# Output projection of a cross-attention block by Strassen's seven block products per head pair, on one Trainium2 core

## The reference, cut to what matters

```python
x = x + xattn(layernorm(x), ctx)       # x, ctx: (16, 256, 512)
    q, k, v = x @ Wq / sqrt(128), ctx @ Wk, ctx @ Wv   # 16 heads of 128
    c = softmax(q @ k.T) @ v           # (16, 256, 16*128)
    return c @ Wo                      # Wo: (2048, 512)
x = x + ffn(layernorm(x))              # gate, up, silu, down, 512 -> 2048 -> 512,
                                       # operands quantised in blocks of 32
```

## Time and profile before

| | us |
|---|---|
| median of 3 runs (lowest, highest) | 2065.28 (2062.91, 2065.92) |
| the profiled execution | 2064.3 |
| its span, first to last instruction | 2062.7 |

### The profile page before, as it was taken

The page is one execution under the profiler, slowest core; times in us unless marked ns, Lnnn a source line. Parts: engine busy times, 40 slices in busy tenths (PEclk is TensorE's granted clock), DMA queues, the critical chain, the costliest instruction groups (busy, mean ns, idle before and its releaser), DMA issues. The chain is left out here.

```text
span 2062.7 us, 45755 instructions
## 1 busy us (share of the span) xinstructions
PE 2023.9 (98%) x15430; PEld 1506.2 (73%) x15430; DVE 1537.7 (75%) x3339; ACT 1000.6 (49%) x2683; POOL 740.0 (36%) x882
## 2 busy tenths in 40 slices
PE   7999999999999999999999999999999999999998
PEld 6778888788888888878888888888888874444443
DVE  6667777777777777778777777776656558888886
ACT  7865545455555555545555545555555453222232
POOL 5322333333323233333332333331111006777776
PEclk9999999999999999999999999999999999999999
DMA  7734444444444444444444444433333273454554
GB/s 234 201 85 83 90 90 90 87 88 89 91 90 90 91 90 91 89 82 90 89 90 91 90 91 88 90 83 75 70 70 69 55 169 77 81 88 86 88 88 79
DMA packets 455038, 193.26 MB, mean 94 GB/s; under 512 B 418400, under 2 KB 431200, under 8 KB 454848
## 3 DMA queue, kind: packets, MB, share of 16 engines
q1 hardware_dynamic: 432496, 139.26, 35.1%
q0 software_dynamic: 16016, 45.23, 9.0%
q10 hardware_dynamic: 6336, 6.29, 1.0%
HBM read 61.21 MB, written 27.26 MB: 43 GB/s over the span
## 5 line engine op out<-in xcount | busy, mean ns | idle before, releaser
L1091 PE MATMUL b_qk<-kvT,attn_weights 128*128 128x256 f16 x3072 | 377.1, 273 | 13.0 <-DVE qk L760 12.3
L651 ACT ACTIVATE prob<-b_s,nmax 128x256 f32<-128x256 f32 x514 | 239.3, 470 | 290.8 <-DVE nmax L921 290.8
L1091 PE MATMUL b_qk<-xT,attn_weights 128*128 128x256 f16 x3072 | 377.2, 273 | 0.0
L1091 PE MATMUL b_v<-attn_weights,kvT 128*128 128x256 f16 x3072 | 377.2, 273 | 0.0
L1091 PEld LDWEIGHTS b_qk<-kvT,attn_weights 128*128 128x128 f16 x3072 | 299.5, 98 | 104.6 <-issue 18.9
L948 DVE SCALAR_TENSOR_TENSOR psplit<-prob,rrec,psplit 128x256 f16<-128x256 f32 x514 | 306.4, 637 | 79.2 <-ACT psplit L661 79.2
L760 DVE SCALAR_TENSOR_TENSOR qk<-b_qk,qk 128x512 f16<-128x512 f32 x256 | 176.7, 690 | 246.3 <-ACT qk L610 236.6
L610 ACT ACTIVATE qk<-b_qk 128x512 f16<-128x512 f32 x256 | 152.5, 596 | 422.5 <-PE b_qk L1091 422.2
L1091 PEld LDWEIGHTS b_qk<-xT,attn_weights 128*128 128x128 f16 x3072 | 300.6, 98 | 34.7
L1091 PEld LDWEIGHTS b_v<-attn_weights,kvT 128*128 128x128 f16 x3072 | 300.6, 98 | 34.8
L661 ACT ACTIVATE psplit<-prob,rrec 128x256 f16<-128x256 f32 x514 | 233.0, 500 | 68.7 <-DVE rrec L941 68.7
(11 more groups left out here) (132 smaller groups left out, 2643.7 us busy)
## 6 DMA issues: line engine op xcount, KB each, us to landing
ffn_w<-wffn SPq DMA_DIRECT2D x48, 256.0 KB, 2.8
acc<-xtok POOLq DMA_DIRECT2D x16, 512.0 KB, 4.9
out<-acc POOLq DMA_DIRECT2D x16, 512.0 KB, 3.2
xrow<-xtok POOLq DMA_DIRECT2D x31, 256.0 KB, 3.2
out<-attn_weights POOLq DMA_DIRECT2D x31, 256.0 KB, 4.4
kvrow<-kvt POOLq DMA_DIRECT2D x61, 128.0 KB, 2.4
stage<-wattn SPq DMA_DIRECT2D x12, 512.0 KB, 4.0
ffn_scratch<-ffn_t SPq DMA_DIRECT2D x48, 128.0 KB, 2.3
```

What stands on the lines that cost most here:

```text
L651: last = eng.activation(half(prob, q, 256), half(bS, q, 256), ACT.Exp, bias=nmax[:, q:q + 1], scale=1.0, accum_out=rsum[:, q:q + 1])
L1091: last = eng.matmul(out, l, r, start=(a == 0), stop=(a == len(pairs) - 1))
```

## The change

From batch 2 on (`FAST`), the projection of a head pair is no longer 2 x 2 x 2 block products but Strassen's seven, m1 to m7, each of a 128 x 128 combination of context blocks and a 128 x 256 combination of weight blocks, each still three matmuls. The seven products are summed over the batch's 8 pairs in PSUM (`b_pt`, `b_x`, `b_o`, half of `b_w`), and DVE adds them with their signs into `acc`, 12 additions of 256 columns per batch in three groups.

- Context: ACT evicts it whole as f32 into `blocks` (in place of `cbuf`, L106); POOL forms five sums per pair in three instructions (`left_sums`), ACT writes the hi of all seven combinations (`left_hi`, 896 columns), DVE their lo (`left_lo`, 896 columns); the lo of the context (`cbuf`, twice per pair) goes.
- Weights: in batch 1 SP loads the 8 pairs' weights again, POOL, ACT and DVE form and split seven combinations of each (`out_sums`, `out_hi`, `out_lo`; 1792 columns per pair) and SP stores them to DRAM. Later SP brings 6 of 8 pairs back for each batch, in two loads of 512 and 384 KB, into two alternating slots; two pairs stay.
- The quantisation of feed-forward weights moves from quads 4 to 51 to quads 8 to 55. Its code, and that around it, is otherwise the same, but for `store_x1`, which POOL issues one quad later.
- Gate and up use `b_qk`, `b_s`, `b_v`, `b_c`; the steps between attention and feed-forward are reordered; the last additions come one per half tile.

The diff, cut to its core, eight columns of indentation and blank lines left out. Left out are buffer layouts, `slot_w`, `left_part` and the like (views of the new buffers), and loop bounds.

```diff
-FFN_FROM, FFN_TO = QPB, QPB + FFN_TILES
+FFN_FROM, FFN_TO = 2 * QPB, 2 * QPB + FFN_TILES
...
+FAST = 2
+FAST_PAIR, FAST_HEAD = 8 * FAST, 16 * FAST
+PREP = (0, 4, 1, 2, 3, 5, 6, 7)
+RESIDENT = {0: 0, 4: 1}
+RING = {1: 2, 2: 3, 3: 2, 5: 3, 6: 2, 7: 3}
+PART_COLS = (2048, 1536)
...
+LEFT = {"a0": 0, "b1": 1, "a0+b1": 2, "a0+b0": 3, "a1+b1": 4, "b0-b1": 5, "a0-a1": 6}
+TERMS = (("m1", "a0+b1", 3), ("m3", "a0", 2), ("m4", "b1", 1), ("m2", "a1+b1", 0)), \
+    (("m5", "a0+b0", 4), ("m7", "b0-b1", 6), ("m6", "a0-a1", 5))
+OPENS, CLOSES = ("m1", "m4", "m5", "m6"), ("m3", "m2", "m7", "m6")
...
-gate = [bPT, bQK]
-up = [bX, bV]
+gate = [bQK, bS]
+up = [bV, bC]
+product_at = {"m1": bPT[:, 0:256], "m3": bPT[:, 256:512], "m4": bX[:, 0:256], "m2": bX[:, 256:512],
+              "m5": bO[:, 0:256], "m7": bO[:, 256:512], "m6": bW[:, 0:256]}
...
+def slot_use(u):
+    b, p_ = u // 8 - FAST, u % 8
+    if p_ in RESIDENT:
+        return RESIDENT[p_], 1
+    uses = [v for v in RING if RING[v] == RING[p_]]
+    return RING[p_], b * len(uses) + uses.index(p_) + 1
...
+    def load_out(j):
+        c, pc = (PREP[j] // 2 + 1) % QPB, O_AT[PREP[j] % 2]
+        eng.dma_start(wall_ffn[:, :], wattn[c * PIECES + pc]).then_inc(sm["wo_loaded"], 16)
+    def store_out(j):
+        eng.wait_ge(sm["wo_lo"], j + 1)
+        eng.dma_start(wos[PREP[j]], wo_split).then_inc(sm["wo_stored"], 16)
+    def load_slot(u, part):
+        slot, _ = slot_use(u)
+        at = slot * 3584 + part * PART_COLS[0]
+        eng.wait_ge(sm["wo_stored"], 16 * (PREP.index(u % 8) + 1))
+        eng.dma_start(oall[:, at:at + PART_COLS[part]],
+                      wos[u % 8, :, part * PART_COLS[0]:part * PART_COLS[0] + PART_COLS[part]]
+                      ).then_inc(sm[f"slot_loaded{slot}{part}"], 16)
...
+    begin = {0: 2 * 1 + 6, 4: 2 * 3 + 6, 1: 2 * 5 + 6, 2: 2 * 6 + 6}
+    fills = {}
+    for p_, step in begin.items():
+        for part in range(2):
+            fills.setdefault(FAST_HEAD - 16 + step + part, []).append((FAST_PAIR + p_, part, FAST_HEAD - 20 + step))
...
+    def fill(i):
+        for u, part, done in fills.get(i, ()):
+            eng.wait_ge(sm["o_done"], done)
+            load_slot(u, part)
...
+            transpose_p(i, k % 2)
...
+            if i == 4 * QPB - 1:
+                load_out(0)
+            if QPB <= n < 2 * QPB and k % 2:
+                j = 2 * (n - QPB) + k // 2
+                store_out(j)
+                if j < 7:
+                    load_out(j + 1)
+            fill(i)
...
+    def out_sums(j):
...
+        eng.tensor_tensor(wo_sums[:, 0:2, :], wo_rows[:, 2:4, :], wo_rows[:, 0:2, :], ALU.subtract
+                          ).then_inc(sm["wo_sum"], 1)
+        eng.tensor_tensor(wo_sums[:, 2:4, :], wo_rows[:, 0:4:2, :], wo_rows[:, 1:4:2, :], ALU.add
+                          ).then_inc(sm["wo_sum"], 1)
+        eng.tensor_tensor(wo_cross, wo_rows[:, 0, :], wo_rows[:, 3, :], ALU.add).then_inc(sm["wo_sum"], 1)
+    def left_sums(n, k):
+        wait_apart(eng, "c_hi", 4 * n + k + 1)
...
+        eng.tensor_tensor(blocks[:, 4:6, :], blocks[:, 1:9:7, :], blocks[:, 0:4:2, :], ALU.add
+                          ).then_inc(sm["s_sum"], 1)
+        eng.tensor_tensor(blocks[:, 6:8, :], blocks[:, 0:2, :], blocks[:, 2:9:6, :], ALU.subtract
+                          ).then_inc(sm["s_sum"], 1)
+        eng.tensor_tensor(blocks[:, 3, :], blocks[:, 1, :], blocks[:, 2, :], ALU.add).then_inc(sm["s_sum"], 1)
...
+            fast = not isinstance(s, int) or 4 * n >= FAST_HEAD + 4
+            if fast:
+                left_sums(n, 0)
+            if outs:
+                out_sums(2 * q)
             if prepare:
                 prep(n, 2 * s + q // 2, q % 2)
+            if outs:
+                out_sums(2 * q + 1)
+            if fast:
+                left_sums(n, 2)
+            if q == 1 and not first_s:
+                store_x1(s - 1, slot)
             if ffn:
                 round_ffn(n - FFN_FROM)
             if q == 0 and not first_s:
-                store_x1(s - 1, slot)
                 if not isinstance(s, int) or s > 1:
                     x_rescale(2 * s - 3)
...
+    left_sums(NQ, 0)
     x_rescale(2 * B - 3)
+    left_sums(NQ, 2)
...
-            if last_batch and v == 0:
+            if last_batch and v == 3:
                 store_x1(B - 1, acc[:, 0:2 * D].rearrange("p (t d) -> p t d", t=2))
...
-        eng.wait_ge(sm["o_done"], 4 * quads - 4)
...
+    def evict_rows(n, k):
+        i = 4 * n + k
+        eng.wait_ge(sm["c_done"], i + 1)
+        if k % 2 and not (isinstance(n, int) and i == FAST_HEAD + 3):
+            eng.wait_ge(sm["s_lo"], 2 * n + (k - 3) // 2 - FAST_PAIR)
+        at = blocks[:, 1:9:7, :] if k % 2 else blocks[:, 0:4:2, :]
+        eng.activation(at, bC[:, 0:256].rearrange("p (q f) -> p q f", q=2), ACT.Copy, scale=C_OUT
+                       ).then_inc(sm["c_hi"], 1)
+    def left_hi(n, k):
+        u = 2 * n + k // 2 - 2 - FAST_PAIR
+        eng.wait_ge(sm["s_sum"], 3 * (u + 1))
...
+        eng.activation(left_part(k // 2, 0).rearrange("p (n f) -> p n f", f=P), blocks[:, 1:8, :], ACT.Copy,
+                       scale=1.0).then_inc(sm["s_hi"], 1)
...
+    def out_hi(j):
+        eng.wait_ge(sm["wo_sum"], 3 * (j + 1))
...
+        to = wo_part(0)
+        eng.activation(to[:, 0:5:4, :], wo_rows[:, 0:4:3, :], ACT.Copy, scale=W_SCALE)
+        for a in range(2):
+            eng.activation(to[:, 1 + 4 * a:3 + 4 * a, :], wo_sums[:, 2 * a:2 * a + 2, :], ACT.Copy, scale=W_SCALE)
+        eng.activation(to[:, 3, :], wo_cross, ACT.Copy, scale=W_SCALE).then_inc(sm["wo_hi"], 1)
...
-            if front or k < 3:
+            if (front or k < 3) and fast(n, k, 3):
+                evict_rows(n, k)
+            elif front or k < 3:
                 hi(half(cbuf, 2 * head_slot(k), 256), bC[:, 0:256], C_OUT, "c_done", i + 1, "c_hi")
...
+            if (front or k < 3) and k % 2 == 0 and fast(n, k, 4):
+                left_hi(n, k)
+            if isinstance(n, int) and n == NQ and k == 2:
+                silu(0, 1)
+            if outs and k % 2:
+                out_hi(2 * (n - QPB) + k // 2)
...
+    def left_lo(n, k):
+        eng.wait_ge(sm["s_hi"], 2 * n + k // 2 - 1 - FAST_PAIR)
+        eng.tensor_tensor(left_part(k // 2, 1).rearrange("p (n f) -> p n f", f=P), blocks[:, 1:8, :],
+                          left_part(k // 2, 0).rearrange("p (n f) -> p n f", f=P), ALU.subtract
+                          ).then_inc(sm["s_lo"], 1)
+    def out_lo(j):
+        eng.wait_ge(sm["wo_hi"], j + 1)
+        to, hi_part = wo_part(1), wo_part(0)
+        pairs = [(to[:, 0:5:4, :], wo_rows[:, 0:4:3, :], hi_part[:, 0:5:4, :])]
...
+        for dst, rows, above in pairs:
+            last = eng.scalar_tensor_tensor(out=dst, in0=rows, scalar=W_SCALE, in1=above,
+                                            op0=ALU.mult, op1=ALU.subtract)
+        last.then_inc(sm["wo_lo"], 1)
...
+    def add_products(b, group):
+        c = b - FAST
+        if group == 0:
+            eng.wait_ge(sm["o_done"], 16 * b + 15)
+            eng.wait_ge(sm["acc_loaded"], 16 * (b + 1))
+        elif group == 2:
+            eng.wait_ge(sm["o_done"], 16 * b + 16)
+        sums = ((("m1", 1, 0, 0), ("m1", 1, 1, 1), ("m3", -1, 0, 1), ("m3", -1, 1, 1)),
+                (("m4", 1, 0, 0), ("m4", 1, 1, 0), ("m2", -1, 1, 1), ("m2", 1, 1, 0)),
+                (("m5", -1, 0, 0), ("m5", 1, 0, 1), ("m6", -1, 1, 1), ("m7", 1, 0, 0)))[group]
+        first_wait = {0: (None, None, None, 2), 1: (0, 0, 0, 2), 2: (0, 0, 0, 1)}[group]
+        for at, (name, sign, tile_, side) in enumerate(sums):
+            if first_wait[at] is not None:
+                eng.wait_ge(sm["m_step"], 12 * c + 4 * group + first_wait[at])
+            a = acc[:, bass.ds(((b + 1) & 1) * (2 * D) + tile_ * D + side * 256, 256)]
+            eng.scalar_tensor_tensor(out=a, in0=product_at[name], scalar=sign * O_OUT, in1=a, op0=ALU.mult,
+                                     op1=ALU.add).then_inc(sm["m_step"], 1)
+        eng.wait_ge(sm["m_step"], 12 * c + 4 * group + 4)
+        if group == 2:
+            eng.sem_inc(sm["o_added"], 2)
+        eng.sem_inc(sm["m_added"], 1)
...
-            if front or k < 3:
+            if (front or k < 3) and not fast(n, k, 3):
                 at = 2 * head_slot(k)
                 lo(half(cbuf, at + 1, 256), bC[:, 0:256], half(cbuf, at, 256), C_OUT, "c_hi", i + 1, "c_lo")
...
+            if (front or k < 3) and k % 2 == 0 and fast(n, k, 4):
+                left_lo(n, k)
+            if isinstance(n, int) and n == NQ and k == 0:
+                inner(0, 0)
+            if isinstance(n, int) and n == NQ and k == 2:
+                inner(0, 1)
+            if outs and k % 2:
+                out_lo(2 * (n - QPB) + k // 2)
             if front and q == QPB and k == 3:
-                add_rows(s, 0)
-            if q == 1 and k == 0 and (not isinstance(s, int) or s > 0):
+                if not isinstance(s, int) or s >= FAST:
```

(49 more changed lines are left out.)

214 lines of the change are left out of this document (116 added, 98 removed).

## The result

The changed kernel takes **2104.9 us** (median of 4 runs, 2104.6 to 2105.5) against 2064.6 for the kernel before: a ratio of **1.0195, 95% interval 1.0179 to 1.0211**. Slower, by 40 us where 26 were forecast. The profiled execution took 2105.04 us, its span 2103.5.

The account below looks back on a forecast made before the run. PE bounds the kernel before; DVE's chain was to take over in batches 2 to 13. 2064.3 + 19.2 - 4.6 + 5.0 + 6.0 = 2089.9, median 1.0 above: 2091 us; whole range 2033 to 2132, forecast's own 2067 to 2119.

Parts of the forecast that it names:

- PE stays the bound: Rival, chance 0.26: removing `cbuf` lo shortens DVE's chain in full, to 100.1 us per batch under PE's 102.3; 2044 us.
- the loads: Rival, chance 0.06: block-weight loads on the transposes' queue hold up the probabilities, 84 us, 2175 us; the forecast took nothing.
- DVE and POOL do block each other: Rival, chance 0.18: half the `left_lo` wait out a POOL instruction, 5.2 us per batch in place of 2.0; 2129 us.
- the tail: End of the attention: last two pairs' chain before PE can project, and late additions, +6 us, bounds 0 and 10.
- batch 15: Without quantisation DVE's chain is 88.9 us and PE stays the bound: -2.3 us, as in batch 14.
- The sum of 106.2 us: DVE's chain per batch, 92.4 + 8.7 + 3.6 - 0.5 + 2.0, over PE's 102.3; +19.2 us in batches 2 to 13.
- `left_lo` +8.7 and additions +3.6: DVE per batch: eight 896-column los of 1.09 us, and 12 additions of 0.415 us in place of two.
- Removal of `cbuf` lo: DVE per batch: removing 6.6 us of work mostly turns busy time into waiting, -0.5 us, bounds 0 and -6.6.
- Contention: `left_lo` meets the last 0.5 us of POOL's work four times a batch: +2.0 us, bounds 0 and 3.7.
- Semaphore waits among the additions: DVE's waits on its own semaphores between additions: 0 to 2.3 us per batch, taken at 0.
- the signs named beforehand: PE 95 to 97% busy waiting at `b_qk`; `rsum` wait up by most of 6 us; batches 14, 15 at 102.3 us.
- adds no time of its own: PE's wait for `m_added` at the first `project` after a batch's end: nothing of DVE depends on it, so no cost.

Follow-up runs that it names:

- run 6: Changed kernel with product m6 taken twice per head pair, 3 more matmuls of 256 columns: 2109.9 us, ratio 1.0219.
- run 5: Changed kernel with POOL's sums, `left_lo`, the additions and the block-weight loads all cut down: 2043.5 us, ratio 0.9897.
- run 1: Changed kernel reordered on DVE alone, `left_lo` right behind the probabilities' lo and additions ahead of other feed-forward work: 2105.9 us, ratio 1.0197.
- run 2: Changed kernel with POOL's three sums on 4 of 128 columns of each block after the first pair: 2071.6 us, ratio 1.0034.
- runs 9, 10 and 12: Changed kernel, full computation, DVE work reordered and resident feed-forward loads spread one per head over batch 15's last twelve heads: 2073.3, 2069.0 and 2073.4 us.
- Run 10: Changed kernel, DVE's scales moved into a wait, additions paired, magic numbers behind `left_lo` in one quad per batch, resident loads spread: 2069.0 us, ratio 1.0023.

## Why the prediction was right, point by point

**Direction and mechanism held.** DVE's chain replaced PE as the bound of batches 2 to 13 (run 6: PE's own work does not set their pace; run 5: with less work on DVE and POOL, PE is full again); batch 14 gained what was forecast (102.2 us against 102.3). Of the rivals, "PE stays the bound" fell, and the loads cost 7 us where that rival had 84. DVE and POOL do block each other, by 3.6 us per batch (below), between the forecast's 2.0 and that rival's 5.2, but not where both put it. The forecast is some 15 us short by the table: 6 in batches 2 to 13 (24.8 against 19.2), 6 in the tail, 3 in batch 15 and 1 in batch 1.

**The sum of 106.2 us came out in part by luck: two terms are wrong and cancel.** Measured is 106.7 us per batch by the window's count (batches 3 to 13 take 107.05 in the mean, 106.75 without the two at a lower clock, see the last section), less 0.7 that DVE still waits for q and k (6.9 us of 1000): 106.0. By terms, each per batch:
- `left_lo` +8.7 and additions +3.6: measured 8 x 1.085 and 12 x 0.415 less the two of the earlier trace rows, as forecast.
- Removal of `cbuf` lo, forecast -0.5: its 6.6 us went, but the wait at `rsum` rose from 35.9 to 70.3 us of 1000, 3.7 us per batch. So **-2.9**. The step "mostly turns busy time into waiting" was a little over half right.
- Contention, forecast +2.0 and only on `left_lo`: DVE's busy time rose by 9.3 us per batch (772.30 x 0.1046 = 80.8 to 844.56 x 0.1067 = 90.1), of which 8.7 + 3.6 - 6.6 = 5.7 is the change's own work. The rest, **+3.6**, is stretching, and not where I put it: `left_lo` itself kept 1.085 us; `rsum` (170 to 384 ns) and the magic numbers (882 ns, 420 in run 1) pay. The meeting that the forecast costed does take place, but POOL pays for it (rows below).
- Semaphore waits among the additions, taken at 0: 4.7 us of 1000 ahead of `qk`, **+0.5**.

The rows of that meeting, from the changed kernel's timeline:

```profile
417.50 1.55 POOL L554 TENSOR_SCALAR ffn_magic_rounded<-ffn_magic_rounded 128x512 f32<-128x512 f32 x1 [0.20 <-POOL ffn_magic_rounded L552]
417.50 1.08 DVE L1070 TENSOR_TENSOR stage<-cbuf,stage 128x896 f16<-128x896 f32 x1
```

POOL's instruction took 0.61 us in the earlier trace rows, and its mean over the middle rose from 684 to 1376 ns, while `left_lo` lost nothing. The two wrong terms are also partly the same microseconds, for the stretched magic numbers fill the wait at `rsum`. In run 2, where they take 432 ns, that wait is 84.2 us of 1000, or 8.8 per batch against 7.5. By this estimate some 1.3 us per batch would leave both terms, and both would be nearer to the forecast.

**The step that failed in size is the tail**: +12.1 us where 6 were forecast, bounds 0 to 10. The forecast had the work of POOL, ACT and DVE on the last pairs covered by one or two gate and up products. One stands ahead of pair 126, and PE still waits 2.59 us there; the second comes only behind the last contexts, since its banks are now those of scores and context. The changed kernel's tail (timelines of PE and DVE, then the windows of its first 60 us, before and changed):

```profile
1732.85 1.44 PE L1359 MATMUL b_pt<-out_weights,stage 128*128 128x256 f16 x6 [2.59 <-DVE stage L1070]
...
1753.44 1.40 DVE L1104 SCALAR_TENSOR_TENSOR acc<-b_x,acc 128x256 f32<-128x256 f32 x4
1755.07 0.69 DVE L984 TENSOR_TENSOR attn_weights<-b_v,attn_weights 128x512 f32<-128x512 f32 x1 [0.22 <-DVE acc L1104]
...
1755.82 1.08 PE L1300 MATMUL b_qk<-attn_weights,out_weights 128*128 128x512 bf16 x4 [3.33 <-DVE attn_weights L984]
```

```profile
1690.30:1750.30 60.00, 58.62 (x306) 29.36 (x305) 46.70 (x87) 21.49 (x50) 32.39 (x24) 1.00 0.42 95
...
1719.00:1779.00 60.00, 49.86 (x278) 27.60 (x276) 41.78 (x80) 20.53 (x45) 26.08 (x23) 0.94 0.37 91
```

The last line of the timeline is the product waiting for DVE's `inner` (L984), late behind the second group of additions. PE is idle for 10.1 of these 60 us where it was idle for 1.4: that is 8.8 of the 12.1 us. Most of the rest is the clock, 0.94 in this window (60 x 0.06 = 3.6 us by estimate), for which the forecast has no term. With all four parts light the tail is 376.4 us, and the clock stays at 1.00 in the like window, so 8 of the 12 us go with them, the clock's among these, and 4 remain. That the banks are what keeps the cover away was read from the code and the order of PE, not tried.

**Batch 15 is the other wrong term**: -2.3 us forecast, +0.3 measured, since the loads, costed at nothing, meet the resident weights there; with those spread (runs 9, 10 and 12) the fifteen steps take 95.6 us, 2.4 less than before. Batch 1 (+5.7, forecast +5.0) held.

**Of the signs named beforehand**, PE at 95 to 97% (96.7 in 400 to 1300 us), DVE's wait at q and k near zero, `left_lo` at 1.1 us and batch 14 at 102.2 us with PE full came true. Not so: PE does not wait at `b_qk` but at the projection, the wait at `rsum` grew by 3.7 us per batch, not by most of 6, and `left_lo` takes no longer where it meets POOL. That PE's wait for the additions "adds no time of its own" held in the main: run 1 more than halved it and the time stayed. The exception is the clock, which fell after two of these waits (last section).

**Why no version beat the kernel before.** Run 10 reaches the last head's start 6.1 us earlier than before (1684.2 against 1690.3 us), and gives 9.3 us back in the tail (381.7 against 372.4). Its PE timeline there:

```profile
1698.04 0.81 PE L1368 MATMUL b_pt<-out_weights,stage 128*128 128x256 f16 x6 [2.59 <-DVE stage L1074]
...
1718.85 1.04 PE L1309 MATMUL b_qk<-attn_weights,out_weights 128*128 128x512 bf16 x4 [2.69 <-DVE attn_weights L988]
```

The same two waits, in an order that left PE 14 us of standing in the middle 1000 where the changed kernel has 34.

## What to carry to other kernels

A cheaper product on the engine that is full pays only as far as the next engine's chain has room, and that chain is its work plus the waits that nothing fills: sum both, take the sum stretch by stretch rather than as a mean, and test it by giving the first engine its work back, which should then cost nothing. Put new work of a late engine into a wait that it has anyway, and don't take work out of one. Look at the end of the stage separately: work that hides in a steady loop stands bare behind its last turn, the more so, as the code suggests here, when buffers were taken from what used to run there. And count the clock: an engine that is made to wait can come back slower.
